# Twenty shared feed-forward groups inside the attention stage, and respaced sends to the experts, in a one-layer language-model tower

## The chip, the core and the metric

The kernel runs on one core of one Trainium2 chip. The metric is device time in microseconds (us), where lower is better. A profile of one more execution is read beside it; its times count from the first instruction.

Five engines work from queues of their own: TensorE (PE; its weight loads are PEld), VectorE (DVE), ScalarE (ACT), GpSimd (POOL) and SyncE (SP). SP only issues transfers here. POOL issues the indirect ones, which gather or scatter rows by a list of indices.

## What is computed

16,384 tokens (128 sequences of 128) of 128 features pass an embedding table, one attention layer and one feed-forward layer. That layer is the sum of a shared two-layer network and two banks of eight experts, of which each token uses one per bank. Cut to its core:

```python
h = table[x]                                    # rows under 250 are sines of a number
h = h + attention(layernorm(h))                 # 8 heads, heads mixed before and after softmax
x2 = layernorm(h).reshape(16384, 128)

def bank(x2, Wr, br, W1, b1, W2, b2):           # 8 experts, at most 1280 tokens each
    probs = softmax(x2 @ Wr + br)
    expert, gate = argmax(probs), max(probs)
    pos = (cumsum(one_hot(expert)) * one_hot(expert)).sum(-1) - 1
    keep = pos < 1280
    slot = expert * 1280 + minimum(pos, 1279)
    buf = zeros(8 * 1280, 128).at[slot].add(where(keep, x2, 0))
    out = gelu(buf @ W1 + b1) @ W2 + b2         # per expert, 128 -> 512 -> 128
    return out[slot] * gate * keep

shared = gelu(x2 @ Ws1 + bs1) @ Ws2 + bs2       # the same widths, every token
h = h + shared + bank(x2, *sp) + bank(x2, *fq)
```

## The kernel before

A tile is 128 tokens, and a group is two tiles (`GROUP`, 256 tokens). Four stages follow each other, each a block of instructions with a barrier behind it.

**Setup** makes the embedding table and the folded attention matrices.

**Attention** (`attention`) runs the 128 tiles through one software pipeline, a step per tile. It also routes the tokens: every eight tiles make a batch, and `routed` counts batches whose target rows are known. POOL then sends each tile's normalized rows (`x2`) by two indirect DMAs (`send`), one to the buffer of each bank in DRAM, `sent_sp` and `sent_fq`. The last sixteen tiles (`LATE` = 112 and up) send to the first bank alone here.

In steps 129 to 139, past the last tile, the pipeline has room. There it computes the shared network of the first `HEAD` = 8 groups, the *head groups*. The tables `AFTER`, `BEHIND` and `BESIDE` say at which step PE, DVE and ACT run which head stage. In stage n PE transposes group n (`head_turned`), runs the first layer of group n - 1 (`head_up`) and the second layer of group n - 2 (`head_down`). ACT applies gelu in between, and DVE normalizes, splits into high and low parts and adds the result to `h_sb`.

**Experts** (`experts`) runs 80 groups, forty per bank. In step k PE transposes group k + 1, runs the first layer of group k (12 matmuls, `up`) and the second layer of group k - 1 (16 matmuls, `down`). DVE adds the bias into `res` (`out`). POOL scatters the two halves of `res` by token into `answers_sp` or `answers_fq` with two indirect DMAs (line 1658). In the steps of `LATE_AT`, each second one from step 1 to step 31, POOL also issues one of the sixteen sends to the second bank that attention left over. SP loads the groups' rows and the next experts' weights.

**Shared** (`shared_ffn`) runs the shared network for the other 56 groups from the transposed rows that attention kept (`turned`), and combines. In step k PE runs the first layer of group k and the second of group k - 1. DVE weights the two answers by the gates, adds them to `h_sb` (`part`, four instructions) and adds PE's result (`res`). SP loads `xT` four steps ahead and both answers (`sh_back`) two steps ahead, and stores `res` to `out`.

The sixteen tiles of the head groups have their shared result already; they still have to be combined. They go one by one, every third step from step 4 (`HEADS_FROM`, `head_tile`). For *head tile* n SP loads both answers into `one_back` (line 1732) in the step that `head_tile` names. DVE combines them into `one_part` and `one_out` two steps later, in the instructions on lines 1833 and 1836, and SP stores `one_out` (line 1746) three steps after the load. There are two buffers of `one_back` and of `one_out`, taken in turn. So three waits tie the head tiles together:

```python
need(sp, S["one_out"], n - 1)                 # load n: tile n - 2 has been combined
need(dve, s_one_put[n % 2], n // 2 * 16)      # combine n: the store of tile n - 2 has landed
need(sp, S["one_out"], n + 1)                 # store n: tile n has been combined
```

Each engine, SP too, works through its instructions in program order. In a step SP issues `xT`, then the head tile's two loads, then two `sh_back` loads, then the store of `res`, and last the store of a head tile.

Of the kernel before, what the change touches and what calls it, by code (L numbers as in the profile page):

```python
# [28 lines left out]
TILES = B * N // P  # L29
# [7 lines left out]
BANKS = 2  # L37
# [5 lines left out]
INV_TWO_PI = 0.15915494309189535  # L43
ROUND = 12582912.0
PI_BELOW = 3.1415925
HEAD = 8
ZERO_ROWS = 10
FILLS = ROWS // P // ZERO_ROWS
DROPPED = 1 << 20
# [699 lines left out]
def attention(nc, bank, shared, first, C, table, sent, ident, h_sb, ids, gates, norm2,  # L749
# [4 lines left out]
    with ExitStack() as s:  # L754
# [48 lines left out]
        ws1_hi, ws1_lo = w_hi[0][:, 0, 0:FC, :], w_lo[0][:, 0, 0:FC, :]  # L803


        AFTER = {129: (0,), 130: (1,), 131: (2,), 132: (3,), 136: (4,), 138: (5,), 139: range(6, HEAD + 2)}
        BEHIND = {129: (0,), 130: (1,), 131: (2,), 134: (3,), 137: (4,), 139: range(5, HEAD + 2)}
        BESIDE = {129: (0,), 131: (1,), 132: (2,), 133: (3,), 135: (4,), 137: (5,), 139: range(6, HEAD + 2)}
        names = ("head_w", "head_hi", "head_made", "head_turned", "head_xhi", "head_xlo", "head_up", "head_gelu",
                 "head_down", "head_out", "scored", "copied", "maxed", "expd", "rtot", "normed", "turned", "turn_out", "u_made", "u_out",  # L810
# [4 lines left out]
        s_got = [sem(f"a_got{k}") for k in range(8)]  # L815
        s_late = sem("a_late_put")


        FETCHED_AT = {-2: range(OWN, 8), 2: (8, 9, 10), 3: (11,), 4: (12, 13, 14)}
        RESID_AT = {4: (), 5: (8, 9, 10), 6: (11, 12, 13)}  # L820
# [36 lines left out]
        @block.sync  # L857
        def _(sp):
            t_main = table[0:P * VR, :].rearrange("(p r) d -> p (r d)", p=P)
            for n, c in enumerate(ORDER[ON_TIME:]):  # L860
                sp.wait_ge(S["late_done"], n + 1)
                sp.dma_start(t_main[:, chunk_cols(c)], h_sb[:, chunk_cols(c)]).then_inc(s_late, 16)
            W1, b1, W2, _ = shared

            for b in range(BANKS):
                z_t = sent[b].rearrange("(p n r) d -> n p (r d)", p=P, r=ZERO_ROWS)
                for n in range(FILLS):
                    sp.wait_ge(S["scored"], 6 + (b * FILLS + n) * 2 // 3)
                    sp.dma_start(z_t[n], zeros[:, :, :].rearrange("p r d -> p (r d)")).then_inc(s_zeroed, 16)

            load_expert(sp, bank, 0, first, first.loaded)
            sp.dma_start(bs1_c[:, :], b1.rearrange("(c p) -> p c", p=P), allow_slow_non_contiguous=True).then_inc(S["head_w"], 16)

            def clear(n):
                a_t = answers[n // CLEARS].rearrange("(p n r) d -> n p r d", p=P, r=CLEAR_ROWS)
                sp.dma_start(a_t[n % CLEARS], zeros[:, 0:CLEAR_ROWS, 0:D]).then_inc(s_cleared, 16)

            for q in range(QUADS):
                sp.wait_ge(S["x2T"], q + 1)
                sp.dma_start(turned[q], x2T[q % 2][:, :]).then_inc(s_kept[q % 2], 16)  # L880
                clear(q)
                if q == QUADS - 3:
                    sp.wait_ge(S["x_made"], GROUPS)
                    sp.wait_ge(S["resid"], TILES)
                    sp.dma_start(ws1, W1.rearrange("p (f c) -> p f c", f=FC)).then_inc(S["head_w"], 16)
                    sp.dma_start(ws2, W2.rearrange("(c p) d -> p c d", p=P)).then_inc(S["head_w"], 16)
            for k in range(2):
                sp.wait_ge(s_kept[k], 16 * QUADS // 2)
            for k in range(8):
                sp.wait_ge(s_sent[k], TILES // 16 * 64 - 32)  # L890
            for a in range(AHEAD):
                sp.dma_start(rows[a][:, :, :], sent[0][a * GROUP:(a + 1) * GROUP, :].rearrange("(s p) d -> p s d", p=P)).then_inc(s_in[a], 16)

        @block.gpsimd
        def _(pool):
# [32 lines left out]
            def step(i, k):  # L928
                j = k % 4

                if k == 4:
                    deviations(i, k)
                if live(i, k - 2):
                    need(pool, S["rtot"], tile(i, k - 1))
                    need(pool, S["turned"], tile(i, k - 3))
                    if k == 2:
                        pool.wait_ge(S["x_made"], 3)
                    nc.gpsimd.tensor_tensor(prob[k % 2][:, :].rearrange("p (g j) -> p g j", g=H),  # L938
                                            expd[k % 2][:, :].rearrange("p (g j) -> p g j", g=H),
                                            rtotal[k % 2][:, :].unsqueeze(2).to_broadcast([P, H, N]),  # L940
                                            ALU.mult).then_inc(S["normed"], 1)

                if k == 2:
                    first_deviations(2, S["stat1"], S["rstd"])

                if k == -3:
                    pool.wait_ge(S["w_made"], 1)
                    residuals(range(OWN))

                for t in FETCHED_AT.get(k, (k + 10,) if 4 <= k < TILES - 10 else ()):  # L950
                    if t == OWN:
                        pool.wait_ge(s_late, 16 * LATES)
                    if t % 4 == 0:
                        for b in range(4):
                            need(pool, s_got[(t + b) % 8], landed(i, t - 8 + b))
                        link(nc.gpsimd.tensor_copy(gi[(t // 4) % 2][:, :], ids[:, t:t + 4]))
                    need(pool, S["x_made"], group(i, t - 8) + 1)
                    need(pool, S["resid"], t - 7)
                    nc.gpsimd.indirect_dma_start(  # L959
                        got[t % 8][:, :], None, table,  # L960
                        bass.IndirectOffsetOnAxis(ap=gi[(t // 4) % 2][:, t % 4:t % 4 + 1], axis=0),
                    ).then_inc(s_got[t % 8], 16)
                    if t + 1 in RESID_BEHIND:
                        residuals(RESID_BEHIND[t + 1])

                residuals(RESID_AT.get(k, (k + 7,) if 7 <= k < TILES - 7 else ()))

                if k == -1:
                    first_deviations(0, S["first_stat"], S["first_rstd"])

                if j == 0 and k > 4 and (live(i, k + 4) or live(i, k - 8)):
                    deviations(i, k)

                if live(i, k - 20):
                    t = k - 20
                    if isinstance(i, int) and t == 0:

                        pool.wait_ge(s_zeroed, 16 * BANKS * FILLS)
                    need_apart(pool, S["routed"], batch(i, t) + 1)
                    late = isinstance(i, int) and tile(i, t) >= LATE  # L980
                    for b in range(1 if late else BANKS):
                        send(nc, sent, x2, to_row, t, b, s_sent[t // 2 % 8])

            pipelined(pool, step, BODY, FIRST, LAST, LEAD, END, link, PCHAIN)
            for k in range(8):
                pool.wait_ge(s_sent[k], TILES // 16 * 64 - 32)

        @block.tensor
        def _(pe):
# [476 lines left out]
def experts(nc, banks, first, sent, x2, to_row, answers, ident, h_sb, res, tokens, rows, s_in, turned, xT, s_x, xT_parts, s_scattered, s_cleared):  # L1466
# [6 lines left out]

    LOOPS = ((1, E // 2 - 1), (E // 2 + 1, PAIRS - 1))
    LOADS = 64
    LATES = TILES - LATE

    LATE_AT = tuple(range(1, 1 + 2 * LATES, 2))
    with ExitStack() as s:
        def sb(n, shape, dt=F32):  # L1480
            return s.enter_context(nc.sbuf_tensor(f"ex_{n}", shape, dt))
# [8 lines left out]
        ps_x = [s.enter_context(nc.psum_tensor(f"ex_ps_x{k}", [P, 512], F32)) for k in range(2)]  # L1490
        ps_h = [s.enter_context(nc.psum_tensor(f"ex_ps_h{k}", [P, FC, G], F32)) for k in range(2)]
        ps_o = [s.enter_context(nc.psum_tensor(f"ex_ps_o{k}", [P, 512], F32)) for k in range(2)]
        S = {n: sem(n) for n in ("turned", "xhi", "xlo", "up", "gelu", "down", "out", "late", "next_hi")}
        S["w_hi"], S["w_lo"] = first.s_hi, first.s_lo
        bs2_b, s_bs2 = sb("bs2_b", [P, D]), sem("bs2")
        s_w = [first.loaded, sem("loaded")]
# [33 lines left out]
        def _(sp):  # L1530
# [3 lines left out]
            def step(i, k, bank):  # L1534
# [8 lines left out]
                if live(i, a) and a >= AHEAD:  # L1543
                    b = bank_of(i, a, bank)
                    need(sp, S["xlo"], group(i, a) - RING + 1)
                    if isinstance(i, int) and group(i, a) == GROUPS:
                        sp.wait_ge(S["late"], 16 * LATES)
                    src = sent[b][bass.ds((group(i, a) - b * GROUPS) * G, G), :]
                    sp.dma_start(rows[a % RING][:, :, :], src.rearrange("(s p) d -> p s d", p=P)).then_inc(s_in[a % RING], 16)

# [97 lines left out]
        def _(pool):  # L1648
            pool.wait_ge(s_cleared, 16 * BANKS * CLEARS)

            def step(i, k, bank):
                if isinstance(i, int) and k in LATE_AT:
                    send(nc, sent, x2, to_row, LATE + LATE_AT.index(k), 1, S["late"])
                if live(i, k - 1):
                    r, b = (k - 1) % RING, bank_of(i, k - 1, bank)
                    need_apart(pool, S["out"], group(i, k))
                    for half in range(2):
                        nc.gpsimd.indirect_dma_start(  # L1658
                            answers[b], bass.IndirectOffsetOnAxis(ap=tokens[r][:, half:half + 1], axis=0),
                            res[r][:, half, :], None, bounds_check=B * N - 1, oob_is_err=False).then_inc(s_scattered[r], 16)  # L1660
# [4 lines left out]
def shared_ffn(nc, first, answers, turned, h_sb, gates, xT, s_x, xT_parts, res, s_scattered, out):  # L1665
# [5 lines left out]
    with ExitStack() as s:  # L1671
# [31 lines left out]
        def dram_rows(t, i, k):  # L1703
            return t[bass.ds((group(i, k) + HEAD) * G, G), :].rearrange("(s p) d -> p s d", p=P)

        HEADS_FROM = 4

        def head_tile(i, k):

            n = (k - HEADS_FROM) // 3  # L1710
            return (n, n) if (k - HEADS_FROM) % 3 == 0 and 0 <= n < 2 * HEAD else None

        @block.sync
        def _(sp):
# [151 lines left out]
```

## Time and profile before

| | us |
|---|---|
| median of three runs | 1514.55 |
| lowest and highest run | 1514.14, 1516.37 |
| span of the profiled execution | 1551.0 |
| setup, about | 69 |
| attention, its tail with the head groups included, about | 1000 |
| experts, about | 297 |
| shared, about | 182 |

The page gives no other time of the profiled execution than its span. Timeline rows read: start, duration, engine, line, operation, output<-inputs, count; the bracket gives the idle time before the row and what ended it. "remote" stands for a semaphore that no instruction of the profile is seen to have set just then. A row's matmuls overlap, so the start of the next row, and not the duration, tells the pace.

### The profile page before, as it was taken

The page shows a single profiled execution, that of the slowest core. Times are in us where ns is not written, and L with a number is a line of the kernel's source. Part 1 is how long each engine was busy: PE and PEld are TensorE (multiplying, and loading weights), DVE is VectorE, ACT ScalarE, POOL GpSimd, SP SyncE. Part 2 cuts the span into 40 slices and gives each one's busy share as a digit, 9 for nine tenths or more (in the row PEclk, how much of TensorE's full clock was granted, in tenths as well). Part 3 has the DMA queues.
Part 4 walks back from the last instruction along what each step waited for, and adds up shares of the span by engine and source line. Part 5 has one row for each costly group of instructions (what it writes and reads, how often), then busy time and mean ns, then how long its engine had stood idle before and what let it go on. Part 6 is the DMA issues. An engine that isn't in the chain of part 4 may idle for free. (4 is left out here: it accounts for less than half of the span.)

```text
span 1551.0 us, 33789 instructions
## 1 busy us (share of the span) xinstructions
PE 1486.1 (96%) x11128; PEld 1370.1 (88%) x11128; DVE 1049.6 (68%) x2810; ACT 1148.1 (74%) x3470; POOL 969.7 (63%) x998
## 2 busy tenths in 40 slices
PE   6789999999999999999999999978889999999999
PEld 3479999999999999999999999877888999999999
DVE  7977787788788788778788787642333343346666
ACT  6788888888888888888888888844444555556655
POOL 7575568887887887887887886643566566520000
PEclk9999999999999999999999999989999999999999
DMA  7224412112111111111111110112333323456665
GB/s 261 114 74 160 145 40 68 48 48 59 38 40 58 37 35 56 34 34 48 43 34 37 54 34 26 58 45 56 75 94 83 85 72 87 120 153 190 184 191 146
DMA packets 171503, 126.48 MB, mean 82 GB/s; under 512 B 30309, under 2 KB 154959, under 8 KB 171330
## 3 DMA queue, kind: packets, MB, share of 16 engines
q1 hardware_dynamic: 153794, 104.15, 22.7%
q0 software_dynamic: 17536, 20.17, 4.7%
q8 instruction: 91, 1.49, 0.4%
q14 instruction: 82, 0.67, 0.1%
HBM read 61.64 MB, written 78.66 MB: 90 GB/s over the span
## 5 line engine op out<-in xcount | busy, mean ns | idle before, releaser
L1138 ACT ACTIVATE expd<-masked,nmax 128x128 f32<-128x128 f32 x1024 | 395.9, 393 | 0.2 <-DVE nmax L1286 0.2
L938 POOL TENSOR_TENSOR prob<-expd,rtotal 128x1024 f32<-128x1024 f32 x128 | 243.2, 1900 | 126.8 <-DVE rtotal L1255 121.3
L1275 DVE COPY_PREDICATED masked<-off_diag,ps_s 128x1024 f32<-128x1024 int32 x128 | 174.7, 1365 | 143.5 <-PE ps_s L1031 143.5
L1071 PE MATMUL ps_o<-u,probT 128*128 128x128 f32 x2048 | 249.1, 275 | 0.0
L1071 PEld LDWEIGHTS ps_o<-u,probT 128*128 128x128 f32 x2048 | 239.0, 191 | 0.0
L1138 ACT ACTIVATION_READ_ACCUMULATOR expd<-masked,nmax 128x1 f32 x1024 | 196.6, 192 | 0.0
L1147 ACT ACTIVATE u<-ps_ut 128x1024 f32<-128x1024 f32 x128 | 131.4, 1026 | 66.5 <-PE ps_ut L1082 55.2
L1162 ACT ACTIVATE probT<-ps_ut 128x1024 f32<-128x1024 f32 x128 | 131.5, 1027 | 45.5 <-PE ps_ut L1039 37.9
L1231 DVE TENSOR_TENSOR w_lo<-ps_w,w_hi 128x512 fp32r<-128x512 f32 x256 | 164.4, 681 | 0.9 <-ACT w_hi L1171 0.9
L1171 ACT ACTIVATE w_hi<-ps_w 128x512 fp32r<-128x512 f32 x256 | 146.2, 596 | 15.9 <-PE ps_w L1057 9.3
L1286 DVE TENSOR_REDUCE nmax<-masked 128x8 f32<-128x1024 f32 x128 | 155.6, 1216 | 2.4
L1055 PE MATMUL ps_w<-xT_hi,M_hi 128*128 128x256 f32 x512 | 154.2, 301 | 3.1 <-DVE xT_lo L1225 2.2
L744 POOL DMA_INDIRECT sent_fq<-x,to_row x128 | 125.9, 983 | 50.0 <-issue 38.7
L744 POOL DMA_INDIRECT sent_sp<-x,to_row x128 | 131.0, 1024 | 37.1 <-issue 23.9
L1056 PE MATMUL ps_w<-xT_hi,M_lo 128*128 128x256 f32 x512 | 143.5, 280 | 0.0
L1794 ACT ACTIVATE sh_hid<-sh_ps_h,b 128x256 f32<-128x256 f32 x224 | 87.8, 474 | 75.2 <-PE sh_ps_h L1766 70.2
L1057 PE MATMUL ps_w<-xT_lo,M_hi 128*128 128x256 f32 x512 | 143.4, 280 | 0.0
L959 POOL DMA_INDIRECT got<-table,gi x124 | 126.3, 1019 | 24.8 <-issue 12.6
L1039 PEld LDWEIGHTS ps_ut<-ident,prob 128*128 128x128 f32 x1024 | 116.1, 141 | 25.4 <-issue 15.6
L1039 PE MATMUL ps_ut<-ident,prob 128*128 128x128 f32 x1024 | 134.0, 274 | 3.4 <-ACT u L1147 2.3
L1658 POOL DMA_INDIRECT answers_sp<-res,tokens x80 | 81.8, 1022 | 63.5 <-DVE res L1637 42.7
L1658 POOL DMA_INDIRECT answers_fq<-res,tokens x80 | 80.8, 1010 | 55.3 <-DVE res L1637 34.9
(252 smaller groups left out, 3914.8 us busy)
## 6 DMA issues: line engine op xcount, KB each, us to landing
turned<-x2T SPq DMA_DIRECT2D x32, 256.0 KB
answers_sp<-zeros SPq DMA_DIRECT2D x16, 512.0 KB
answers_fq<-zeros SPq DMA_DIRECT2D x16, 512.0 KB
xT<-turned SPq DMA_DIRECT2D x56, 128.0 KB
sh_back<-answers_sp SPq DMA_DIRECT2D x56, 128.0 KB, 2.3
sh_back<-answers_fq SPq DMA_DIRECT2D x56, 128.0 KB, 2.5
out<-res SPq DMA_DIRECT2D x56, 128.0 KB, 2.1
h_sb<-in_L_tok_weight SPq DMA_DIRECT2D x12, 512.0 KB, 6.2
```

Of the source, the lines that this page charges most:

```text
L744: nc.gpsimd.indirect_dma_start(sent[b], bass.IndirectOffsetOnAxis(ap=to_row[(t // BATCH) % 2][:, c:c + 1], axis=0), x2[:, t % 16, :], None ...
L938: nc.gpsimd.tensor_tensor(prob[k % 2][:, :].rearrange("p (g j) -> p g j", g=H), expd[k % 2][:, :].rearrange("p (g j) -> p g j", g=H), rtot ...
L1039: mm = nc.tensor.transpose(ps_ut[:, g * N:(g + 1) * N], prob[(k - 3) % 2][:, g * N:(g + 1) * N], ident[:, :])
L1055: nc.tensor.matmul(o, M_hi, xT_hi[:, m % 4, :], start=True, stop=False)
L1056: nc.tensor.matmul(o, M_lo, xT_hi[:, m % 4, :], start=False, stop=False)
L1071: mm = nc.tensor.matmul(ps_o[:, 0:D], probT[k % 2][:, g * N:(g + 1) * N], u[k % 2][:, g * D:(g + 1) * D], start=(g == 0), stop=(g == H - 1))
L1138: ins = nc.scalar.activation(expd[(k - 1) % 2][:, g * N:(g + 1) * N], masked[(k - 1) % 2][:, g * N:(g + 1) * N], ACT.Exp, bias=nmax[(k - 1 ...
L1171: nc.scalar.activation(w_hi[m % 2][:, :, 2 * q:2 * q + 2, :].rearrange("p b g j -> p g b j"), ps_w[q % 2][:, :].rearrange("p (g b j) -> p ...
L1231: nc.vector.tensor_tensor(dst, ps_w[q % 2][:, :].rearrange("p (g b j) -> p g b j", g=2, b=2), hi.bitcast(F32), ALU.subtract).then_inc(S["w ...
L1275: nc.vector.copy_predicated(masked[k % 2][:, :].rearrange("p (g j) -> p g j", g=H), off_diag[:, :].unsqueeze(1).to_broadcast([P, H, N]), p ...
L1286: nc.vector.tensor_reduce(nmax[k % 2][:, :], masked[k % 2][:, :].rearrange("p (g j) -> p g j", g=H), X_AXIS, ALU.max, negate=True).then_in ...
L1658: nc.gpsimd.indirect_dma_start(answers[b], bass.IndirectOffsetOnAxis(ap=tokens[r][:, half:half + 1], axis=0), res[r][:, half, :], None, bo ...
```

## The change

1. `HEAD` is 20. Attention computes the shared network of twenty groups, and the shared stage that of 44. `AFTER` and `BEHIND` are shifted by a step or two.
2. Tiles below `LATE` are sent as before. The last sixteen tiles' sends, now 32 for both banks, come in a loop of their own (`late_sends`) behind POOL's other attention work. Each waits for a place in the head groups: even ones for `head_up`, odd ones for `head_turned`, one count further every second send, from counts 2 and 4 on. The experts send nothing any more, and SP's wait for those sends goes.
3. In the experts, the scatter of the second half of group k - 1 waits for the first layer of group k + 1 (`up`).
4. In the shared stage the head tiles, now 40, go one per step from step 2 (`HEADS_FROM` = 2) instead of one in every third step.

```diff
-HEAD = 8
+HEAD = 20
...
-        AFTER = {129: (0,), 130: (1,), 131: (2,), 132: (3,), 136: (4,), 138: (5,), 139: range(6, HEAD + 2)}
-        BEHIND = {129: (0,), 130: (1,), 131: (2,), 134: (3,), 137: (4,), 139: range(5, HEAD + 2)}
+        AFTER = {129: (0,), 130: (1,), 131: (2,), 132: (3,), 135: (4,), 136: (5,), 138: (6,), 139: range(7, HEAD + 2)}
+        BEHIND = {129: (0,), 130: (1,), 131: (2,), 134: (3,), 135: (4,), 137: (5,), 139: range(6, HEAD + 2)}
...
+        SENDS_FROM = HEAD - 2 - (TILES - LATE)
...
-                sp.wait_ge(s_sent[k], TILES // 16 * 64 - 32)
+                sp.wait_ge(s_sent[k], TILES // 16 * 64)
...
-                    need_apart(pool, S["routed"], batch(i, t) + 1)
-                    late = isinstance(i, int) and tile(i, t) >= LATE
-                    for b in range(1 if late else BANKS):
-                        send(nc, sent, x2, to_row, t, b, s_sent[t // 2 % 8])
+                    if t < LATE:
+                        pool.wait_ge(S["routed"], batch(i, t) + 1)
+                        for b in range(BANKS):
+                            send(nc, sent, x2, to_row, t, b, s_sent[t // 2 % 8])
+
+            def late_sends():
+                for n in range((TILES - LATE) * BANKS):
+                    q, b, e = n // BATCH // BANKS, n // BATCH % BANKS, n % BATCH
+                    t = LATE + q * BATCH + e
+                    if e == 0:
+                        pool.wait_ge(S["routed"], t // BATCH + 1)
+                    if n % 2 == 0:
+                        pool.wait_ge(S["head_up"], n // 2 + SENDS_FROM)
+                    else:
+                        pool.wait_ge(S["head_turned"], n // 2 + SENDS_FROM + 2)
+                    send(nc, sent, x2, to_row, t, b, s_sent[t // 2 % 8])
...
-                    if isinstance(i, int) and group(i, a) == GROUPS:
-                        sp.wait_ge(S["late"], 16 * LATES)
...
-                if isinstance(i, int) and k in LATE_AT:
-                    send(nc, sent, x2, to_row, LATE + LATE_AT.index(k), 1, S["late"])
                 if live(i, k - 1):
                     r, b = (k - 1) % RING, bank_of(i, k - 1, bank)
                     need_apart(pool, S["out"], group(i, k))
                     for half in range(2):
+                        if half:
+                            need(pool, S["up"], group(i, k) + 2, ALL)
...
-        HEADS_FROM = 4
+        HEADS_FROM = 2
...
-            n = (k - HEADS_FROM) // 3
-            return (n, n) if (k - HEADS_FROM) % 3 == 0 and 0 <= n < 2 * HEAD else None
+            n = k - HEADS_FROM
+            return (n, n) if 0 <= n < 2 * HEAD else None
```

What stands on three queues at the places that count is shown next. Each row is an instruction, with its line, its output<-inputs and the semaphores it waits for.

SP in the middle of the shared stage before: one step with a head tile, between steps without one.

```order
L1719 DMA xT3<-turned 128x256 [waits sh_xlo]
L1732 DMA sh_one_back0_1<-answers_sp 128x128 [waits sh_one_out]
L1732 DMA sh_one_back1_1<-answers_fq 128x128
L1738 DMA sh_back0_1<-answers_sp 128x2x128 [waits sh_part]
L1738 DMA sh_back1_1<-answers_fq 128x2x128
L1742 DMA out_0<-res0 128x2x128 [waits sh_out]
L1746 DMA out_0<-sh_one_out0 128x128 [waits sh_one_out]
L1719 DMA xT0<-turned 128x256 [waits sh_xlo]
L1738 DMA sh_back0_2<-answers_sp 128x2x128 [waits sh_part]
L1738 DMA sh_back1_2<-answers_fq 128x2x128
L1742 DMA out_0<-res1 128x2x128 [waits sh_out]
```

The same place after:

```order
L1729 DMA xT0<-turned 128x256 [waits sh_xlo]
L1742 DMA sh_one_back0_0<-answers_sp 128x128 [waits sh_one_out]
L1742 DMA sh_one_back1_0<-answers_fq 128x128
L1748 DMA sh_back0_2<-answers_sp 128x2x128 [waits sh_part]
L1748 DMA sh_back1_2<-answers_fq 128x2x128
L1752 DMA out_0<-res1 128x2x128 [waits sh_out]
L1756 DMA out_0<-sh_one_out1 128x128 [waits sh_one_out]
L1729 DMA xT1<-turned 128x256 [waits sh_xlo]
L1742 DMA sh_one_back0_1<-answers_sp 128x128 [waits sh_one_out]
L1742 DMA sh_one_back1_1<-answers_fq 128x128
L1748 DMA sh_back0_3<-answers_sp 128x2x128 [waits sh_part]
```

Seven transfers now stand in every step, where there were seven in each third step and four in the others.

DVE in the same stage before, around the end of a step without a head tile (`sh_one_put` tells that a head tile's store has landed):

```order
L1819 SCALAR_TENSOR_TENSOR sh_part1<-sh_back1_1,gates,sh_part1 128x128 [waits sh_half]
L1819 SCALAR_TENSOR_TENSOR sh_part1<-sh_back1_1,gates,sh_part1 128x128
L1825 TENSOR_TENSOR res1<-sh_ps_o1,sh_part1 128x256 [waits sh_part,sh_put1,sh_down]
L1805 TENSOR_TENSOR sh_xT_lo0<-xT0,sh_xT_hi0 128x256 [waits sh_xhi]
L1813 SCALAR_TENSOR_TENSOR sh_part0<-sh_back0_2,gates,h_sb 128x128 [waits sh_back2,sh_out]
```

And after:

```order
L1829 SCALAR_TENSOR_TENSOR sh_part0<-sh_back1_0,gates,sh_part0 128x128
L1835 TENSOR_TENSOR res0<-sh_ps_o0,sh_part0 128x256 [waits sh_part,sh_put0,sh_down]
L1843 SCALAR_TENSOR_TENSOR sh_one_part<-sh_one_back0_1,gates,h_sb 128x128 [waits sh_one_out,sh_one_put1,sh_one_back1]
L1846 SCALAR_TENSOR_TENSOR sh_one_out1<-sh_one_back1_1,gates,sh_one_part 128x128 [waits sh_one_part]
L1815 TENSOR_TENSOR sh_xT_lo1<-xT3,sh_xT_hi1 128x256 [waits sh_xhi]
```

The two instructions of a head tile now stand between `res` and the next group's `xT_lo` in every step, and the first of them waits for the store of the tile two before it.

POOL at the end of attention before, with the start of the experts' program behind it:

```order
L912 TENSOR_TENSOR rstd1<-var,power 128x8 [waits a_pchain]
L744 DMA sent_sp<-x2,to_row0 10240x132 [waits a_routed] x8
L744 DMA sent_sp<-x2,to_row1 10240x132 [waits a_routed] x8
L754 UNCONDITIONAL_BRANCH [waits a_sent4,a_sent5,a_sent3,a_sent6,a_sent2,a_sent7,a_sent1,a_sent0]
L1647 UNCONDITIONAL_BRANCH [waits barrier_Pool_Activation_PE_DVE_SP_gather]
L744 DMA sent_fq<-x2,to_row0 10240x132 [waits s_cleared]
L1658 DMA answers_sp<-res0,tokens0 16384x128 [waits ex_out]
L1658 DMA answers_sp<-res0,tokens0 16384x128
```

And at the end of attention after, where the first bank's sends of batch 14 give way to the second bank's:

```order
L744 DMA sent_sp<-x2,to_row0 10240x132 [waits a_head_up]
L744 DMA sent_sp<-x2,to_row0 10240x132 [waits a_head_turned]
L744 DMA sent_fq<-x2,to_row0 10240x132 [waits a_head_up,a_routed]
L744 DMA sent_fq<-x2,to_row0 10240x132 [waits a_head_turned]
L744 DMA sent_fq<-x2,to_row0 10240x132 [waits a_head_up]
```

Two rows of eight sends became 32 sends with a wait each, and the sends between the experts' scatters are gone.

## Rows read from the trace of the kernel before

**Rows 1.** The page: its span, and the chain that ended last, by engine.

```profile
span 1551.0 us, 33789 instructions
PE 25%; another core or an unknown queue 3%; issue 1%; DVE 1%; ACT 1%; DMA 1%; POOL 0%; SPq 0%; POOLq 0%; DVEq 0%; ACTq 0%
```

**Rows 2.** Windows: stretch, length; busy (x instructions) PE, PEld, DVE, ACT, POOL; clock, DMA, GB/s.

```profile
69.00:1020.00 951.00, 940.83 (x6734) 854.51 (x6735) 753.50 (x1960) 821.67 (x2665) 724.99 (x731) 1.00 0.18 55
1020.00:1071.00 51.00, 37.19 (x285) 35.96 (x283) 16.07 (x65) 21.39 (x48) 18.13 (x20) 0.87 0.14 39
1071.00:1184.00 113.00, 100.36 (x818) 96.56 (x819) 37.53 (x121) 52.56 (x140) 65.48 (x66) 0.97 0.36 91
1184.00:1366.00 182.00, 180.28 (x1569) 179.35 (x1569) 68.31 (x215) 101.08 (x261) 107.33 (x107) 1.00 0.35 89
1369.00:1551.00 182.00, 177.98 (x1568) 177.35 (x1568) 115.60 (x366) 104.38 (x278) 2.65 (x3) 1.00 0.62 179
```

**Rows 3.** Timeline of PE in the head groups, two idle times.

```profile
1038.61 0.61 PE L1008 MATMUL ps_o<-wr,x2T 128*128 128x16 f32 x2 [6.06 <-ACT x2T L1153]
...
1062.52 0.55 PE L1107 MATMUL ps_s<-xT_hi,w_hi 128*128 128x256 f32 x1 [5.43 <-ACT masked L1194]
```

**Rows 4.** Timeline of ACT there.

```profile
1060.81 1.57 ACT L1194 ACTIVATE masked<-ps_s,bs_c 128x256 f32<-128x256 f32 x4 [5.28 <-remote]
```

**Rows 5.** Timeline of POOL there: the last send of each row of eight.

```profile
1035.55 0.98 POOL L744 DMA_INDIRECT sent_sp<-x,to_row  x1 [0.30 <-issue]
...
1058.39 0.98 POOL L744 DMA_INDIRECT sent_sp<-x,to_row  x1 [0.31 <-issue]
```

**Rows 6.** Timeline of PE: first layers of two head groups, and of two shared groups.

```profile
1050.19 0.36 PE L1107 MATMUL ps_s<-xT_hi,w_hi 128*128 128x256 f32 x1
...
1053.62 0.36 PE L1107 MATMUL ps_s<-xT_hi,w_hi 128*128 128x256 f32 x1
...
1441.66 0.37 PE L1764 MATMUL sh_ps_h<-sh_xT_hi,w_hi 128*128 128x256 f32 x1
...
1444.82 0.37 PE L1764 MATMUL sh_ps_h<-sh_xT_hi,w_hi 128*128 128x256 f32 x1
```

**Rows 7.** Timeline of SP in the shared stage: a head tile's step, and a slow issue.

```profile
1459.13 0.45 SPq L1732 DMA_DIRECT2D sh_one_back<-answers_sp  x1
1459.61 0.43 SPq L1732 DMA_DIRECT2D sh_one_back<-answers_fq  x1
1460.38 0.37 SPq L1738 DMA_DIRECT2D sh_back<-answers_sp  x1
1460.80 0.46 SPq L1738 DMA_DIRECT2D sh_back<-answers_fq  x1
1461.36 0.42 SPq L1742 DMA_DIRECT2D out<-res  x1
1461.82 0.47 SPq L1746 DMA_DIRECT2D out<-sh_one_out  x1
...
1469.57 1.51 SPq L1738 DMA_DIRECT2D sh_back<-answers_sp  x1
```

**Rows 8.** Timeline of DVE in that step: `res`, then the head tile.

```profile
1457.74 0.42 DVE L1825 TENSOR_TENSOR res<-sh_ps_o,sh_part 128x256 f32<-128x256 f32 x1 [1.23 <-PE sh_ps_o L1775]
1458.09 0.34 DVE L1833 SCALAR_TENSOR_TENSOR sh_one_part<-sh_one_back,gates,h_sb 128x128 f32<-128x128 f32 x1
1458.46 0.35 DVE L1836 SCALAR_TENSOR_TENSOR sh_one_out<-sh_one_back,gates,sh_one_part 128x128 f32<-128x128 f32 x1
```

**Rows 9.** DMA issues of the whole run: count, size, median us from issue to landing.

```profile
out<-sh_one_out SPq DMA_DIRECT2D x16, 64.0 KB, 1.9
```

**Rows 10.** Chain of waits in the experts, the start of a second layer.

```profile
1080.04 1.78 PE ex_ps_o L1585 x16
```

**Rows 11.** Timeline of POOL there, the second half of the group before.

```profile
1080.92 0.98 POOL L1658 DMA_INDIRECT answers_sp<-res,tokens  x1 [0.30 <-issue]
```

**Rows 12.** Windows, as rows 2: a stretch after an idle time of PE.

```profile
1039.00:1045.00 6.00, 6.00 (x30) 6.00 (x30) 2.63 (x10) 1.78 (x5) 0.00 (x0) 0.50 0.43 134
```

More of the change, by code:

```diff
@@ L978, in step @@
                         pool.wait_ge(s_zeroed, 16 * BANKS * FILLS)
-                    need_apart(pool, S["routed"], batch(i, t) + 1)
-                    late = isinstance(i, int) and tile(i, t) >= LATE
-                    for b in range(1 if late else BANKS):
-                        send(nc, sent, x2, to_row, t, b, s_sent[t // 2 % 8])
+                    if t < LATE:
[13 more added lines that the diff above has]
+                    send(nc, sent, x2, to_row, t, b, s_sent[t // 2 % 8])
             pipelined(pool, step, BODY, FIRST, LAST, LEAD, END, link, PCHAIN)
+            late_sends()
             for k in range(8):
-                pool.wait_ge(s_sent[k], TILES // 16 * 64 - 32)
+                pool.wait_ge(s_sent[k], TILES // 16 * 64)
         @block.tensor
@@ L1475, in experts @@
     LOADS = 64
-    LATES = TILES - LATE
-    LATE_AT = tuple(range(1, 1 + 2 * LATES, 2))
     with ExitStack() as s:
@@ L1492, in experts @@
         ps_o = [s.enter_context(nc.psum_tensor(f"ex_ps_o{k}", [P, 512], F32)) for k in range(2)]
-        S = {n: sem(n) for n in ("turned", "xhi", "xlo", "up", "gelu", "down", "out", "late", "next_hi")}
+        S = {n: sem(n) for n in ("turned", "xhi", "xlo", "up", "gelu", "down", "out", "next_hi")}
         S["w_hi"], S["w_lo"] = first.s_hi, first.s_lo
```

## The prediction

> **What bounds the kernel now.** Read the page first: the chain that ended last is TensorE, and its second entry, 3%, is waits that no seen instruction ended [rows 1]. Then cut the span into stages with the windows. In attention, in the later experts and in the shared stage PE is busy for 98 or 99% of the time [rows 2]: there only less work for PE, or a wait that comes to exceed PE's own pace, can move the end. Two stretches differ. In the tail of attention with the head groups PE is busy 37.19 of 51 us, and in the first 113 us of the experts 100.36 [rows 2].
>
> How much do these two lose? The later experts make 1569 matmuls in 182 us, 8.62 per us [rows 2]. At that rate the tail's 285 take 33.1 us and the early experts' 818 take 94.9 us. So 17.9 and 18.1 us are lost, 36.0 in all. The timelines show how. PE stands idle for 6.06 and 5.43 us [rows 3]; ACT, on which it waits, itself waited 5.28 us for a remote release [rows 4], and both engines go on 1 to 3 us after the last of eight sends in a row on POOL has begun [rows 3 to 5]. The early experts are where POOL adds sends to its scatters. In this execution, then, dense runs of indirect DMAs delay the handing over from PE to the others, and that is what the change aims at.
>
> **Are those 36 us in the timed runs?** The profiled span is 1551.0 us [rows 1] and the median 1514.55, so the timed runs are 36.45 us shorter than this execution. The stretches in which PE is 98 or 99% busy cannot shrink much; the idle time can. Setup, 69 us, and these 36.0 us are all there is, and the agreement of 36.0 with 36.45 is close. I take it that the timed runs do not have these waits, or hardly. The other case is a rival.
>
> **Part 1, twenty head groups.** Twelve groups move from the shared stage into attention's tail. A shared group costs 3.16 us of PE (first layer to first layer), a head group 3.43, since it adds the two transposes [rows 6]. Removed: 12 x 3.16 = 37.9 us. Added: 12 x 3.43 = 41.2. Both are on PE, which sets the pace at both places: **+3.3 us**. DVE's and ACT's part of a head group lay under PE's at that same pace. The shifted tables move existing stages by a step; I cost that at nothing, between -2 and +2.
>
> **Part 2, sends among the head groups.** 16 more sends go to the tail and leave the experts. Two per 3.43 us of PE is 2 x 1.28 us of POOL (0.98 and 0.30 of issue, [rows 5]), so POOL keeps up. The last is released when group 18 is transposed, three stages, some 10 us, before PE ends the tail, so SP's row loads stay hidden. It is the density of the later experts, two scatters in each step, and there PE is 99% busy [rows 2]: no new idle time. In the profile this returns up to 36 us, in the timed runs about 0 by the paragraph above.
>
> **Part 3, the second half scatter.** The next group's first layer ends by 1080.04, when the second layer begins [rows 10]; the second half is issued at 1080.92 in any case [rows 11]. The wait is over when POOL gets there: 0. Queued behind it on POOL is only the next group's scatter.
>
> **Part 4, a head tile in every step.** Here I see the price. Two buffers and SP's program order make a ring. SP's loads of head tile n wait until DVE has combined tile n - 2. DVE combines tile n - 1 one step later, and only when the store of tile n - 3 has landed; that store stands last in the very step whose first loads were waiting. Before, with a tile in every third step, the same waits had been over for several steps. Now each step goes through all of: the five issues ahead of the store, the landing of the store, the two DVE instructions, the handing over.
>
> - Issues: from the first load at 1459.13 to the store at 1461.82 is 2.69 us, some 0.3 of it waiting [rows 7]. So 2.4 undisturbed; with a slow issue of 1.51 us among them [rows 7], 3.5. I take 2.7, nearer to the undisturbed step, since most issues take under 0.5.
> - Landing of the store, issue to landing: 1.9 us [rows 9].
> - Combining: 1458.09 to 1458.81, 0.7 us [rows 8].
> - Three handings over: some 0.1 us; `res` shows none larger, since its wait for PE ends with PE [rows 8].
>
> The sum is 5.4 us for a step, with 5.1 and 6.2 as ends, where PE needs 3.16. In the steps before, DVE had 1.23 us to spare [rows 8], and `xT_lo` for PE stands behind the head tile in DVE's queue; so DVE's pace becomes PE's. The ring closes for head tiles 2 to 39: 38 steps x (5.4 - 3.16) = **+85.1 us** (73.7 to 115). Behind the last of them nothing catches up, for DVE ends the stage.
>
> **Sum.** 3.3 + 85.1 = +88.4 us on the timed runs: 1514.55 + 88.4 = **1603 us**. Against the profiled execution: 1551.0 + 88.4 - 36.0, a span of 1603 as well.
>
> **TensorE's clock** is what speaks further against the change. After the idle 6.06 us [rows 3] the granted clock is 0.50, the 1.2 GHz level, though PE is busy throughout: 30 matmuls in 6.00 us [rows 12]. At that rate a group's 28 take 5.6 us, at half of full pace 6.3. In the early experts PE was 89% busy and the clock 0.97 [rows 2]; the new shared step has PE busy for 3.16 of 5.4. If the clock falls in most steps, PE takes the ring's place at about 6.0 us a step: 0.6 x 38 = 23 us more, 1626. The Trainium skill, page "TensorE: Matmul & The Clock Gate", section "HAM oscillation — how this bites in real kernels", describes such a kernel, whose waits for data bring the throttle back before every piece of work. By that rule this rival would be the forecast; the trace shows the fall after one long idle time and not for gaps of 1 or 2 us, and no row has gaps of 2.2 us in every step.
>
> **Rivals.**
> - *The waits are in the timed runs too* and go: 1603 - 36 = 1567. For it: the trace shows them, and nothing in it names the profiler. Against: 36.0 beside 36.45.
> - *The clock falls* in the shared stage: 1626.
> - *The ring stays open and SP's issuing alone sets the pace* (the store would have to land while SP issues the next loads, or DVE not wait for it). Seven transfers at some 0.49 us are 3.4 us, with a share of slow ones 3.7, in 40 steps: +21.6, so 1514.55 + 3.3 + 21.6 = 1539. Against: the wait stands in the queue.
> - *Faster*: the 36 us of late releases in the tail and early experts are real and are freed by the spacing, while the shared stage keeps PE's pace: 1514.55 + 3.3 - 36 = 1482. This decides as long as a step there takes less than 3.16 + 32.7 / 38 = 4.0 us. Five issues and one landing alone exceed that.
> - *The change does not do what it says*: for the scatter's wait I take that for sure (it is over when reached). For the sends: if they still delay PE although spaced, that shows in the profile and adds nothing to the timed forecast.
>
> **How the numbers follow.** Forecast 1603: chance 0.66, its own range 1588 to 1630 from a step of 5.1 to 6.0. Waits real and gone, 1567: 0.15. Clock, 1626: 0.08. SP alone, 1539: 0.05. Faster, 1482: 0.04. What is left, 0.02, lies above 1640. A range of 8 in 10 takes in the forecast, most of the clock and of the waits: 1556 to 1632. A measurement of this kernel can tell about 0.2%, 3 us, from no change; faster by more has 0.04, within it 0.01, slower 0.95.
>
> **What would show it.** In the shared stage: first layers about 5.4 us apart from the seventh group or so on; DVE's line of `one_part` waiting for the transfer `out<-sh_one_out` in every step, some 2 us; SP's `one_back` waiting for DVE in every step; PE's share of that window near 60%. In the tail: head groups 3.43 us apart and no idle time of 5 us. In the early experts: about 8.6 matmuls per us. A shared pace near 3.2 us refutes part 4, near 3.7 leaves SP's issuing. A profiled span that falls by less than 36 us against 1551.0 + 88 says that the spacing failed. A timed result near 1567 with the ring in place says that the waits were in the timed runs.

## The result and the profile after

The changed kernel takes 1602.07 us (median of four runs, 1600.17 to 1602.88). The kernel before, run beside it, takes 1514.35 (1512.91 to 1516.37). The ratio is 1.0578 with a 95% interval of [1.0565, 1.0591]: 87.7 us slower. The forecast was 1603, from +88.4.

The profiled execution of after took 1602.88 us with a span of 1601.2. In every run told below, the time is likewise the span plus about 1.7 us. So a profiled span, with these 1.7 us added, can be set beside the timed runs.

First the page, as [rows 1]: the span, and the chain that ended last, by engine.

```profile
span 1601.2 us, 33901 instructions
DVE 5%; DMA 5%; PE 1%; issue 1%; SPq 1%; DVEq 0%; ACT 0%
```

Before, most of the chain was PE's. Now a transfer and DVE lead it. The windows, with the columns of [rows 2], say in which stage: attention without its tail, the tail with twenty head groups, the experts, the shared stage.

```profile
69.00:1020.00 951.00, 940.17 (x6735) 853.86 (x6736) 754.12 (x1963) 822.03 (x2665) 725.07 (x731) 1.00 0.18 55
1020.00:1094.00 74.00, 72.59 (x636) 71.97 (x635) 29.89 (x106) 43.43 (x106) 33.50 (x35) 1.00 0.11 29
1097.00:1369.00 272.00, 271.63 (x2382) 271.37 (x2383) 104.10 (x332) 155.46 (x400) 158.53 (x156) 1.00 0.38 97
1372.00:1601.00 229.00, 163.89 (x1232) 156.89 (x1232) 110.88 (x342) 81.61 (x218) 2.25 (x3) 0.92 0.47 135
```

The tail and the experts are full of PE work: 98 and 99.9% busy. The experts make 2382 matmuls in 272 us, 8.76 per us, from their first microsecond on. The shared stage is not: 1232 matmuls in 229 us are 5.38 per us, against 8.62 in the same stage of before (1568 in 182, [rows 2]). Nearly all that was lost lies there.

Who waits there? The waits of DVE, of SP's queue and of PE in that stage, each with total us, number, and longest:

```profile
DVE sh_one_part L1843 <- DMA out<-sh_one_out: 97.9, 37, 4.2
SPq L1742 <- DVE sh_one_out L1846: 74.5, 37, 3.7
PE sh_ps_h L1774 <- DVE sh_xT_lo L1815: 58.0, 30, 3.6
```

Read as a circle: DVE waits for the landing of a head tile's store 37 times, SP's load of the next head tile waits for DVE 37 times, and PE's first layer waits for `xT_lo`, which stands behind the head tile in DVE's queue. The timeline of SP shows one turn (start, duration), as [rows 7] did for before:

```profile
1485.80 0.33 SPq L1742 DMA_DIRECT2D sh_one_back<-answers_sp  x1
1486.17 0.43 SPq L1742 DMA_DIRECT2D sh_one_back<-answers_fq  x1
1486.64 0.43 SPq L1748 DMA_DIRECT2D sh_back<-answers_sp  x1
1487.12 0.47 SPq L1748 DMA_DIRECT2D sh_back<-answers_fq  x1
1487.63 0.47 SPq L1752 DMA_DIRECT2D out<-res  x1
1488.15 0.47 SPq L1756 DMA_DIRECT2D out<-sh_one_out  x1
```

And the timeline of DVE, as [rows 8]: two head tiles in a row, with the idle time before each and what ended it.

```profile
1478.54 0.35 DVE L1843 SCALAR_TENSOR_TENSOR sh_one_part<-sh_one_back,gates,h_sb 128x128 f32<-128x128 f32 x1 [2.43 <-DMA out<-sh_one_out]
1478.92 0.35 DVE L1846 SCALAR_TENSOR_TENSOR sh_one_out<-sh_one_back,gates,sh_one_part 128x128 f32<-128x128 f32 x1
...
1485.03 0.35 DVE L1843 SCALAR_TENSOR_TENSOR sh_one_part<-sh_one_back,gates,h_sb 128x128 f32<-128x128 f32 x1 [3.69 <-DMA out<-sh_one_out]
1485.42 0.35 DVE L1846 SCALAR_TENSOR_TENSOR sh_one_out<-sh_one_back,gates,sh_one_part 128x128 f32<-128x128 f32 x1
```

`one_out` ends at 1485.77 and SP's load is issued at 1485.80: the load had been waiting for it. In [rows 8] `one_part` followed `res` at once. `one_part` of head tile 1 starts at 1391.24 and that of tile 38 at 1593.61: 37 steps of 5.47 us on the mean. The forecast was 38 of 5.4.

### The profile page after: what moved, and what is told of

It is laid out like the page before. It is cut to its first block and busy times, and to the rows that moved or that the text cites. A ratio compares the mean times of both kernels' runs of the same rounds, so it can differ in the third digit from the quotient of the medians.

```text
span 1601.2 us, 33901 instructions
## 1 busy us (share of the span) xinstructions
PE 1498.5 (94%) x11152; PEld 1382.0 (86%) x11152; DVE 1059.1 (66%) x2834; ACT 1150.6 (72%) x3470; POOL 970.3 (61%) x998
## 5 line engine op out<-in xcount | busy, mean ns | idle before, releaser
L1804 ACT ACTIVATE sh_hid<-sh_ps_h,b 128x256 f32<-128x256 f32 x176 | 69.0, 475 | 141.9 <-PE sh_ps_h L1776 141.9
L744 POOL DMA_INDIRECT sent_fq<-x,to_row x128 | 125.9, 984 | 46.9 <-issue 37.4
L961 POOL DMA_INDIRECT got<-table,gi x124 | 126.3, 1019 | 24.8 <-issue 12.9
```

What stands on the lines that cost most here:

```text
L744: nc.gpsimd.indirect_dma_start(sent[b], bass.IndirectOffsetOnAxis(ap=to_row[(t // BATCH) % 2][:, c:c + 1], axis=0), x2[:, t % 16, :], None ...
```

## The experiments

Two theories stand against each other on part 4. The *ring*: loads, store, landing and combining follow each other around, and the length of the circle is the step. *SP's issuing*: seven transfers in each step, whatever their order, are too many for SP. A third question is the 36 us of idle time in the trace of before: are they in the timed runs, and do dense runs of indirect DMAs make them?

### The store of the head tile first in SP's step

```diff
             def step(i, k):
+                if head_tile(i, k - 3):
+                    t, n = head_tile(i, k - 3)
+                    need(sp, S["one_out"], n + 1)
+                    sp.dma_start(out[bass.ds(t * P, P), :], one_out[n % 2][:, :]).then_inc(s_one_put[n % 2], 16)
                 a = k + 4
...
-                if head_tile(i, k - 3):
-                    t, n = head_tile(i, k - 3)
-                    need(sp, S["one_out"], n + 1)
-                    sp.dma_start(out[bass.ds(t * P, P), :], one_out[n % 2][:, :]).then_inc(s_one_put[n % 2], 16)
```

> The changed kernel with one thing moved: in each SP step of the shared stage the store of a head tile stands first instead of last. Transfers, sizes and buffers are the same. Theory (the ring of store, landing, combining and the next loads sets the pace): the store no longer stands behind the wait for the tile combined just before, so the ring opens; what is left is SP's issuing, seven transfers a step, some 3.7 us. 38 steps x (5.4 - 3.7) = 64 us less, 1538 us (1530 to 1545), and DVE no longer waits for the store. Rival (the amount of transfers, on SP or on the DMA engines, sets the pace): 1602 us as before.

Measured: 1535.32 us (1534.01 to 1535.94), ratio to before 1.0135 [1.012, 1.0151]. The same transfers, the same number, another place in the queue, and 66.7 of the 87.7 us are gone. Its waits in the shared stage, DVE's and SP's:

```profile
DVE res L1835 <- DMA out<-res: 36.5, 34, 3.1
DVE sh_one_part L1843 <- DMA out<-sh_one_out: 1.1, 1, 1.1
SPq L1756 <- DVE res L1835: 2.6, 4, 1.4
```

The 97.9 us of waiting for a head tile's store are 1.1, and SP hardly waits for anyone any more. What is left is the other theory's case: SP issues without a break, one turn from store to store on its timeline:

```profile
1440.72 0.47 SPq L1735 DMA_DIRECT2D out<-sh_one_out  x1
1441.23 0.45 SPq L1729 DMA_DIRECT2D xT<-turned  x1
1441.72 0.43 SPq L1746 DMA_DIRECT2D sh_one_back<-answers_sp  x1
1442.20 0.43 SPq L1746 DMA_DIRECT2D sh_one_back<-answers_fq  x1
1442.67 0.43 SPq L1752 DMA_DIRECT2D sh_back<-answers_sp  x1
1443.15 0.47 SPq L1752 DMA_DIRECT2D sh_back<-answers_fq  x1
1443.66 0.47 SPq L1756 DMA_DIRECT2D out<-res  x1
1444.17 0.47 SPq L1735 DMA_DIRECT2D out<-sh_one_out  x1
...
1448.81 1.78 SPq L1746 DMA_DIRECT2D sh_one_back<-answers_sp  x1
```

Seven issues take 3.45 us, and now and then one takes 1.78 instead of 0.43. PE needs 3.16. So both costs are real. With the ring closed its length decides; with the ring open SP's issuing costs 18.8 us more than the next experiment, in which SP has time.

### Two head tiles in one transfer, every second step

```diff
-            n = k - HEADS_FROM
-            return (n, n) if 0 <= n < 2 * HEAD else None
+            n = (k - HEADS_FROM) // 2
+            return (n, n) if (k - HEADS_FROM) % 2 == 0 and 0 <= n < HEAD else None
```

The buffers hold two tiles, and the loads, the store and DVE's instructions go over both.

> The changed kernel with the head tiles combined by twos: one load per bank, one combination and one store for two tiles, every second step. The same bytes and the same DVE work, but three transfers for two tiles instead of six, and the waits are over two steps earlier. Theory: ring open and SP at 5.5 transfers a step, 2.7 to 3.0 us, under PE's 3.16; so the shared stage returns to 3.16 us a group and what stays of the change is 12 x (3.43 - 3.16) = 3.3 us: 1517.7 us (1514 to 1523). If the late releases of the kernel before were in the timed runs, their removal would show here: 1482 us. If bytes or DVE set the pace: near 1602 us.

Measured: 1516.56 us (1514.45 to 1517.53, eleven runs), ratio 1.0008 [0.9999, 1.0017]. Parts 1 to 3 of the change are all in it, with all forty head tiles in the shared stage. Its window of that stage, columns as above:

```profile
1372.00:1511.00 139.00, 137.56 (x1214) 136.92 (x1212) 105.76 (x342) 80.95 (x217) 0.00 (x0) 1.00 0.77 220
```

PE is 99% busy at a granted clock of 1.00, and the DMA engines move 220 GB/s where they moved 135 in after. The shared stage of after was therefore not short of bandwidth. What remains is the price of parts 1 to 3 together: 1.6 us on the medians, between none and 2.6 by the interval.

### One issue more inside the ring

```diff
-                a = k + 4
-                if live(i, a) and a >= BACK:
-                    load_x(i, a)
+                if live(i, k + 4) and k + 4 == BACK:
+                    load_x(i, k + 4)
...
+                if live(i, k + 5) and k + 5 > BACK:
+                    load_x(i, k + 5)
                 if head_tile(i, k - 3):
```

> The changed kernel with one transfer's issue moved inside the ring: xT of the next step is issued between the store of res and the store of the head tile, instead of ahead of the next head tile's loads. The number of transfers stays the same. Ring theory: six issues instead of five stand between the loads and the store, 38 steps x 0.48 us = +18.2, 1620. Rival, that the seven issues of a step, and not their place, set the pace: unchanged, 1602.

Measured: 1626.93 us (1625.97 to 1631.54), ratio to before 1.0742 [1.0719, 1.0765]. After stood at 1.0578, so the difference is 0.0164 of 1515 us, 24.8. SP still issues seven transfers a step; one of them now stands between the loads and the store. Its waits, and the turn on SP's timeline:

```profile
DVE sh_one_part L1844 <- DMA out<-sh_one_out: 123.6, 37, 4.4
```

```profile
1483.88 0.32 SPq L1741 DMA_DIRECT2D sh_one_back<-answers_sp  x1
...
1485.71 0.47 SPq L1751 DMA_DIRECT2D out<-res  x1
1486.22 0.47 SPq L1729 DMA_DIRECT2D xT<-turned  x1
1486.73 0.45 SPq L1757 DMA_DIRECT2D out<-sh_one_out  x1
```

From the first load to the store it is 2.85 us here, 2.35 in after's turn. From `one_part` to `one_part` (head tiles 1 to 38) a step takes 6.16 us on the mean, against 5.47 in after. Of these 0.69 us, 0.51 are the added issue, as the ring theory says (means over the steps, load to store: 2.96 and 2.44). Another 0.17 is that the store takes longer to let DVE go, 2.43 us instead of 2.26 (medians 2.41 and 2.03). The expectation, 18.2 us, had only the first; the landing's part, 0.17 x 37 = 6.3, brings it to some 24.5. The rival, unchanged, falls.

### Part 4 alone, on the kernel before

```diff
-        HEADS_FROM = 4
+        HEADS_FROM = 2
...
-            n = (k - HEADS_FROM) // 3
-            return (n, n) if (k - HEADS_FROM) % 3 == 0 and 0 <= n < 2 * HEAD else None
+            n = k - HEADS_FROM
+            return (n, n) if 0 <= n < 2 * HEAD else None
```

> The kernel before with its sixteen head tiles in every step from step 2 instead of every third, part 4 alone. Ring theory: from head tile 2 to 15 a step takes 5.4 us and the 14 steps cost 14 x 2.24 = 31.4 us, 1546. Rival, SP's issuing alone at 3.7 us a step: 14 x 0.54 = 7.6, 1522. Rival, the cost lies in having forty head tiles and not in their density: 1515.

Measured: 1542.13 us (1541.0 to 1542.93), ratio 1.0173 [1.0156, 1.019], +26.6 us. With the sixteen head tiles of before, in every step, the ring is there at once:

```profile
DVE sh_one_part L1833 <- DMA out<-sh_one_out: 34.9, 13, 4.4
SPq L1732 <- DVE sh_one_out L1836: 25.8, 13, 3.8
PE sh_ps_h L1764 <- DVE sh_xT_lo L1805: 20.4, 13, 3.8
```

Thirteen waits each, not the fourteen that I had counted: in the last head tile's step no load stands ahead of the store, and that step takes 2.72 us. Thirteen steps of 5.4 us cost 13 x 2.24 = 29.1. In this trace PE's first layers from group to group, over the thirteen that are slowed, add up to 70.4 us where 13 x 3.16 = 41.1 would do: 29.3 more. The timed difference is 2.7 less than that; this execution reached the shared stage 2.6 us earlier than a profile of before did (first layer at 1329.67 and 1332.30; another such profile has 1333.80). That start varies: in four kernels here that are the same program up to there (after among them) it lies from 1369.48 to 1372.53. Both rivals, 1522 and 1515, are far off.

### The waits of the tail and the early experts

Part 3 alone on the kernel before: the second half scatter waits for the next group's first layer.

```diff
                     for half in range(2):
+                        if half:
+                            need(pool, S["up"], group(i, k) + 2, ALL)
```

> The kernel before with part 3 alone: the second half scatter waits for the first layer of the next group. Theory: the wait is over when POOL gets there, 1514 us, within 2 us. Rival (it thins out POOL's issuing and the timed runs gain): down to 1496 us. Rival (the wait delays scatters): over 1517 us.

Measured: 1514.12 us (1512.86 to 1520.82, eleven runs), ratio 1.0003 [0.9992, 1.0013]. Then the kernel before without its sixteen late sends:

```diff
-                if isinstance(i, int) and k in LATE_AT:
-                    send(nc, sent, x2, to_row, LATE + LATE_AT.index(k), 1, S["late"])
```

> The kernel before without the sixteen late sends to the second bank in the experts: they are left out, so sixteen tiles miss the second bank. Theory (the late releases are in the profiled execution alone): timed 1514 us as before, within 3 us, while the profile's early experts go at 8.6 matmuls per us and its span falls by some 18 us. Rival (they are in the timed runs too): 1496 us.

Measured: 1514.42 us (1512.61 to 1517.26, eleven runs), ratio 1.0001 [0.9992, 1.001], with a span of 1515.2. The timed half of the expectation holds. The other half, that the span of 1551.0 would fall by the 18.1 us of the early experts and stand near 1533, does not: 36 us were gone. And the profile of part 3 alone, which keeps every send where it was, is as short as that, at 1512.3. Two different edits with the same short span speak against either as the cause, and the kernel before was profiled twice more, unchanged.

> The kernel before, unchanged, profiled once more. If the 36 us of late releases belonged to the one execution shown, the span is 1512 to 1516 here, the first 113 us of the experts have a group every 3.42 us and PE has no idle time over 3 us among the head groups. Rival, that profiling this kernel brings them: a span near 1551.

> The same once more: 1512 to 1516 if the late releases come in single executions, near 1551 if they come with every profile of this kernel.

Measured: 1516.65 and 1515.37 us, with spans of 1514.9 and 1513.6. The windows of the second (rows of eight sends in the tail, the last head groups and the start of the experts, the early experts):

```profile
1020.00:1055.00 35.00, 32.25 (x280) 31.20 (x278) 15.13 (x59) 20.25 (x46) 17.90 (x19) 1.00 0.20 57
1055.00:1080.00 25.00, 23.65 (x203) 23.23 (x204) 9.23 (x31) 14.18 (x37) 13.23 (x13) 1.00 0.40 103
1080.00:1148.00 68.00, 68.00 (x599) 68.00 (x598) 27.38 (x88) 38.64 (x101) 50.05 (x51) 1.00 0.39 100
```

The same windows of the execution on which the prediction rests:

```profile
1020.00:1055.00 35.00, 27.87 (x220) 27.21 (x219) 13.78 (x58) 17.30 (x37) 14.33 (x16) 0.85 0.16 48
1055.00:1080.00 25.00, 17.52 (x125) 16.66 (x124) 5.10 (x16) 7.96 (x21) 4.79 (x6) 0.86 0.28 71
1080.00:1148.00 68.00, 60.68 (x511) 58.53 (x509) 23.41 (x74) 31.07 (x83) 42.18 (x42) 1.00 0.32 81
```

One program, two executions: 599 matmuls in 68 us and 511. The waits do not belong to every execution of this kernel. Were the sends less dense? The last of the second row of eight, in the new profile and in [rows 5]'s manner:

```profile
1047.23 0.98 POOL L744 DMA_INDIRECT sent_sp<-x,to_row  x1 [0.31 <-issue]
1048.51 0.98 POOL L744 DMA_INDIRECT sent_sp<-x,to_row  x1 [0.30 <-issue]
1049.80 0.98 POOL L744 DMA_INDIRECT sent_sp<-x,to_row  x1 [0.31 <-issue]
```

They come every 1.28 us, as in [rows 5], while PE has no idle time over 1 us anywhere in that tail. Dense sends thus do not suffice to delay the handing over. What did it in that one execution stays open; it did not come back in any profile here.

## Why the prediction was right

**Are those 36 us in the timed runs?** No, as taken. The comparison (36.0 us lost, 36.45 between span and median) decided whether 36 us came off the sum, and two more profiles of before confirm it. Like set against like it was less close: a run's time is its span plus 1.7 us, so the profiled execution was some 38 us longer than the median, and its span was 36.1 and 37.4 us longer than the two new ones. The sentence ahead of it was not borne out: that dense runs of indirect DMAs delay the handing over. I had tied two things that happened at one time in one execution. It cost the forecast nothing, because part 2 was priced at 0 for the timed runs in either case.

**Part 1**, +3.3 us. The pairs' experiment gives 1.6 for parts 1 to 3 together, and its interval ends at 2.6. So the term was somewhat too large; the pitches themselves (in after 3.44 us a head group, first layers at 1054.80 and 1058.24; 3.16 a shared group) stand. What gives back the difference was not measured apart, and the traces cannot tell it: in three executions of before's program up to there, the start of the shared stage alone differs by up to 4.1 us.

**Part 2**, 0, and **part 3**, 0: the timed experiments with the late sends taken out and with the scatter's wait alone lie within 0.1% of before. The new wait ended an idle time of POOL once in the experts of after:

```profile
POOL answers_fq L1668 <- PE ex_ps_h L1586: 0.3, 1, 0.3
```

**Part 4**, +85.1 us. Setting after's trace beside the second profile of before, the shared stage from its first matmul to the end of the span grows from 1513.6 - 1332.3 = 181.3 to 1601.2 - 1372.5 = 228.7 us with twelve groups fewer: 47.4 + 12 x 3.16 = 85.3. In steps that is 37 x (5.47 - 3.16) = 85.5, one step fewer than counted and each 0.07 us longer. The terms inside the step were less exact than their sum. On the mean over these 37 steps, first load to store is 2.44 us (taken 2.7), store to `one_part` 2.26 (taken 1.9), and `one_part` to the next load 0.77 (taken 0.8 with the handing over). The first was too large, since only four of the 292 transfers that SP issues in after's shared stage took over 1 us. The second was too small: 1.9 is the median to the landing, while the median to DVE's start is 2.03, and in six of the steps it was 2.9 to 3.9. The two errors cancel, so that the sum came out this close is in part luck.

The long steps have a mark in the trace. From head tile 1 to head tile 38 eight packets of 16 KB go over the queue q8, which the page calls instruction. Four start within 0.3 us of the four slow issues. The other four, at 1406.32, 1454.50, 1553.20 and 1575.45, fall between a store and the `one_part` that waits for it, and there this wait is longest, 3.4 to 3.9 us. The view of the DMA queues from 1553 to 1554 us shows one of them (packets, MB, share):

```profile
q8 instruction: 1, 0.02, 5.5%
```

The eight steps with such a packet are together 10.4 us longer than eight steps of the median, 5.17 us. In the kernel with the store first, too, each of the eight issues over 1 us has such a packet beside it. That the packets are the cause was not tested.

The moved store, the added issue and part 4 alone each changed this circle, and each moved the time the way it says and by about the size that its steps give, so the ring is shown, not only argued.

**The clock rival**, 1626. The granted clock does fall: to 0.92 over the shared stage, to 0.89 in its last fifth, and in short stretches to 0.50, the 1.2 GHz level:

```profile
1405.00:1410.00 5.00, 1.45 (x13) 1.26 (x11) 1.25 (x5) 1.42 (x5) 0.00 (x0) 0.87 0.34 99
1410.00:1415.00 5.00, 5.00 (x24) 5.00 (x25) 2.53 (x9) 1.87 (x5) 0.00 (x0) 0.50 0.49 144
...
1550.00:1595.00 45.00, 33.13 (x240) 31.73 (x239) 20.79 (x65) 14.36 (x38) 0.00 (x0) 0.89 0.43 125
```

From 1405 to 1410 us PE was idle for most of the time, and then it was busy throughout at the lower level. Even so, the step inside that stretch, from 1408.72 to 1413.79, took 5.07 us, and in all 37 steps it was the landing of a store that ended DVE's idle time before `one_part`. So the lower clock lies in the ring's shadow. The prediction said that by the rule of the Trainium skill this rival would be the forecast, and that read the page too widely. In the kernel that the Trainium skill describes on the page "TensorE: Matmul & The Clock Gate", section "HAM oscillation — how this bites in real kernels", each piece of work, about 2 us, is shorter than the wait for data behind it. Here it is the other way round: PE's waits are 1.9 us on the mean (58.0 us in 30) and the work between them 3.16, and the clock fell to 0.50 in some stretches and not ahead of every step.

**The rival of SP's issuing**, 1539, is what the kernel with the store first turned into: 1535.32, at 3.69 us a step from `one_part` to `one_part` (rival: 3.7). It was the right price for the case that the ring opens.

## What to carry to other kernels

Where a load waits for a buffer, the consumer waits for a store, and both stand in one in-order queue, write down the circle of waits and add up its length: if it is over the pace of the busiest engine, it is the new pace, whatever the engines' shares say. Where in the queue the store stands can matter more than how many transfers there are; moving one store to the front gave back 66.7 of 87.7 us. And before a stall seen in one profiled execution is aimed at, its span is to be set against the timed runs, and the kernel profiled again.

## What the runs showed of the hardware

- One execution of one program had 36 us of idle time, spread over the tail of attention and the early experts, that two more profiles and all timed runs of it lack. Its cause is open.
- SP issues a transfer every 0.45 to 0.5 us, but in every kernel here 4 to 12 of the 232 to 292 in a shared stage take 1.0 to 2.2 us (1.78 in the row above, where its neighbours take 0.43). In a full queue the 1.35 us more of such an issue are over a third of PE's step of 3.16. In after and in the kernel with the store first, each issue over 1 us has a 16 KB packet of the queue q8 (instruction) beside it. In after, the four such packets that fell between a store and the `one_part` waiting for it stand beside the four longest of these waits.
- With one more load issued just ahead of it, a 64 KB store released DVE 0.17 us later on the mean (2.43 instead of 2.26).
